# Weight blocks and degree counts moved beside a gather, last-stage masks and sums kept in PSUM, squares on ScalarE

## The chip, the cores and the metric

One core of a Trainium2 chip runs the whole program. The metric is the device time of one execution in microseconds (us). Of the kernel before there are three plain runs and one execution under the hardware profiler.

## The reference, cut to what matters

A graph of 100000 nodes with 32 features each (x) and 25000 edges (src, dst sorted, a type of 86, a weight). Four graph layers stand one behind the other, each with a residual and a layer norm over the 32 features:

```
x = layernorm(x + L0(x))   # 10 propagation steps: f = 0.9 * dn * segsum((f*sn)[src], dst) + 0.1 * x
x = layernorm(x + L1(x))   # 4-head attention over the edges of one src, softmax, mean over heads, + bias
x = layernorm(x + L2(x))   # relation layer: basis products, tanh gate, segment sum over dst, relu
x = layernorm(x + L3(x))   # L3(x) = segsum(x[src] * weight, dst) + x
```

Nodes without edges go through the norms alone.

## The kernel before, in words

The 25000 edges lie over 128 partitions with T = 196 edges each, in order of dst. XS and XD hold the rows of x for the source and for the target of each edge. They come by indirect DMAs from GpSimd's queue (POOL), one instruction for one edge column: 128 rows of 32 floats. XS takes 196 such instructions, the node table 196, XD 196. XD's are issued in three portions that fill gaps of POOL's order: columns 0 to XD_EARLY (148) ahead of the gather for list 0, up to XD_MID (186) behind it, and the last ten behind the payload gather.

Only edges whose source row is itself a target can change over the propagation steps. They are put on lists: list 0 has 7 trips here, list 1 has 2 trips, a trip being two halves of CU = 4 columns. `list_gather` (L1516) works a list: VectorE (DVE) fills the index tile cidx for both halves, POOL issues four indirect gathers for a half, DVE waits for their landing, takes the rows and refills the indices of the half for the next trip. What is given as `between` runs on DVE after the first two fills and ahead of the first take. There are two halves, so POOL is never more than eight gathers ahead of DVE.

The order around the first part of the change, on DVE: `sums_of_dst` makes segment sums by 32 scans (L1354) into the tile S; they are copied into FULL (L1688), which has 36 floats for an edge; SyncE (SP) writes FULL to the table full_d (L637). DVE waits for that write, clears the region with a memset of 7200 floats (L1712), and works list 0 from full_d. Then it puts out the list sums (L1722 to L1726); SP writes them and the payload. DVE next builds the weight blocks (L1735 to L1769) and the counts per target (L1773 to L1775), makes list 1 (`make_list`, L1465), and gathers its payload in two trips (L1777, `pay_take`). Some masks and a memset of S later it starts the gather of list 1 from the written list sums (L1792). All propagation steps follow, each waiting for the one ahead.

The last stage puts out the rows by target. It has ROUNDS = 7 rounds of RC = 28 edge columns. In a round DVE expands listed rows in a window (L2177 to L2187), adds them to XS (`add_listed`, L2210), and `out_dst` (L2216) norms XS, multiplies with the edge weight, makes 32 scans of 28 elements into S (L2230), adds twice XD, keeps a part for a row split over partitions (held, L2235), and norms again. `deviation` (L2202) squares on DVE (L2204), sums, and has ScalarE (ACT) take the root. `out_fill` writes half a round's 14 rows into the ring, and POOL scatters them to the output, one indirect DMA for a column (L911). The ring has two halves; a half is filled again when its scatters of the round ahead have landed (s_land). ACT's side of the roots is `take_roots` (L2305).

Of the kernel before, what the change touches and what calls it, by code (L numbers as in the profile page):

```python
# [5 lines left out]
ALU = mybir.AluOpType  # L6
# [62 lines left out]
def gnn_resnorm(nc, x, src, dst, etype, eweight, w1, fc_w, fc_b, bias1, w2, w_comp, w_self, A1w, A1b, A2w, A2b,  # L69
# [53 lines left out]
    with ctx:  # L123
# [304 lines left out]
        ROWS_AHEAD = 8  # L428
        XS_AHEAD, XD_EARLY, XD_MID = 160, 148, 186
        assert CH % 4 == 0 and NG == 7 * ROUNDS == 4 * (SINGLES - 1) + 1 and SINGLES <= 2 * ROUNDS  # L430
# [508 lines left out]
        def mid(ap, n):  # L939

            return ap.unsqueeze(1).to_broadcast([ap.shape[0], n, ap.shape[1]])

        @block.vector
        def _(dve):
# [711 lines left out]
            def carry_run(flat, flags, w=D, last=False):  # L1656

                with rn.trip_loop(2) as i:
# [8 lines left out]

            sums_of_dst = lambda src3, dst3, flat: segment_sums(src3, dst3, D, dmask, dfirst,
                                                                enter=lambda first: carry_run(flat, first))
            spread_of_dst = lambda ends_only=False: spread_back(  # L1670
# [12 lines left out]
            st.seq(V.tensor_tensor(Y3, XS3, bc3(c2[:, :], D), ALU.mult))  # L1683
            sums_of_dst(Y3, S3, S)
            st.do(V.memset(tm[:, :], 1.0))
            st.wait()
            positions(cs, act0, T, dmask, dfirst, tm[:, 0:1])
            st.do(V.tensor_copy(FULL[:, :, 0:D], S3))  # L1688
            st.do(V.tensor_copy(FULL[:, :, D], lcnt[:, 0:T]))
# [19 lines left out]
            st.do(V.tensor_copy(p0[:, :, 3], lq[:, 0:CW]))  # L1709
            dve.wait_ge(s_fullw, 16)  # L1710
            st.do(V.memset(zr[:, :, :], 0.0))
            st.do(V.memset(RB[:, 0:CW * TW], 0.0))  # L1712
            st.wait()
            list_gather(0, cs, 0, lidx2, row_take(0, cs, TW, RB[:, 0:CW * TW], TW, YW, True), 9)

# [18 lines left out]

            for k in range(2):  # L1735
                st.seq(V.tensor_tensor(prod[:, 0:NH * D].rearrange("p (h o) -> p h o", h=NH),
                                       wcat[:, :].rearrange("p (h o) -> p h o", h=NH),
                                       mid(wsd[:, k * D:(k + 1) * D], NH), ALU.mult))
                st.seq(V.tensor_reduce(ua[:, k, :], prod[:, 0:NH * D].rearrange("p (h o) -> p h o", h=NH), AX.X,
                                       ALU.add))  # L1740
            for k in range(2):
                for h in range(NH):
                    m = (k * NH + h) * D
                    st.do(V.tensor_scalar(udiag[:, m:m + D], ident[0:D, 0:D], ua[0:D, k, h:h + 1], None, ALU.mult))
            for j in range(GT):
                r = slice(32 * j, 32 * j + 32)

                st.do(V.tensor_scalar(bd1[r, j * NH * D:(j + 1) * NH * D].rearrange("i (o h) -> i o h", h=NH),
                                      wcat[r, :].rearrange("i (h o) -> i o h", h=NH), 1.0 / NH, None, ALU.mult))

                st.wait()
                st.do(V.tensor_reduce(bdm[r, j * D:(j + 1) * D], bd1[r, j * NH * D:(j + 1) * NH * D].rearrange(
                    "i (o h) -> i o h", h=NH), AX.X, ALU.add))
                for part, w in ((w16[r, 0:NB * D].rearrange("i (o b) -> i o b", b=NB),
                                 wf[r, :].rearrange("i (b o) -> i o b", b=NB)),
                                (w16[r, NB * D:(NB + 1) * D], aw[r, 0:D]),
                                (w16[r, (NB + 1) * D:(NB + 2) * D], aw[r, 2 * D:3 * D])):
                    st.seq(V.tensor_copy(part, w))
                    if j >= 2:
                        st.seq(V.tensor_tensor(part, w, part, ALU.subtract))  # L1760
                st.do(V.tensor_copy(bdy[r, j * D:(j + 1) * D], aw[r, D:2 * D]))

            st.seq(V.tensor_tensor(relf[:, NB:RW], relf[:, NB:RW], b_b2[:, :], ALU.add))
            st.seq(V.tensor_copy(rel3[:, 0, :], relf[:, :]))
            for k in range(2):
                st.seq(V.tensor_tensor(relf[:, :], relf[:, :], rel3[:, k, :], ALU.subtract))
                st.seq(V.tensor_copy(rel3[:, k + 1, :], relf[:, :]))
            st.wait()
            dve.sem_inc(s_wb, 1)  # L1769


            ones_t = ones[:, 0:1].to_broadcast([P, T]).unsqueeze(2)
            segment_sums(ones_t, c3[:, :].unsqueeze(2), 1, dmask, dfirst)  # L1773
            spread_back(c3[:, :].unsqueeze(2), 1, dend, dstf)
            dve.sem_inc(s_sri, 1)  # L1775
            cs = make_list(1, t1w, CW, pb[:, 0:1], float(CW - ZROW))
            list_gather(1, cs, 0, lq, pay_take(1, cs), 1)  # L1777
            list_masks(1)
# [422 lines left out]

            def deviation(x3):  # L2202

                st.seq(V.tensor_tensor(sq3, x3, x3, ALU.mult))  # L2204
                dve.sem_inc(tick, 1)
                st.seq(V.tensor_reduce(half, sq3, AX.X, ALU.add))
                root()
                st.seq(V.reciprocal(inv, half))

            def add_listed(i, y):  # L2210

                xs = chunk(XS, i)
                st.seq(V.tensor_tensor(y, y, cols2(act0, i).unsqueeze(2).to_broadcast([P, RC, D]), ALU.mult))
                st.seq(V.tensor_tensor(xs, xs, y, ALU.add))

            def out_dst(i, y):  # L2216

                part = prods[:, :, :].rearrange("p a b -> p (a b)")[:, 0:RC * D].rearrange("p (t d) -> p t d", d=D)
                sums, xs, xd = (chunk(t, i) for t in (S, XS, XD))
                center(xs)  # L2220
                deviation(xs)
                st.seq(V.tensor_tensor(inv, inv, cols2(ew, i), ALU.mult))
                st.seq(V.tensor_tensor(y, xs, bc3(inv, D), ALU.mult))
                if not (isinstance(i, int) and i == 0):

                    last = S[:, bass.ds(i * (RC * D) - D, D)]
                    st.seq(V.scalar_tensor_tensor(out=y[:, 0, :], in0=last, scalar=dmask[:, bass.ds(i * RC, 1)], in1=y[:, 0, :],
                                                  op0=ALU.mult, op1=ALU.add))
                for d in range(D):
                    st.do(V.tensor_tensor_scan(sums[:, :, d], cols2(dmask, i), y[:, :, d], 0.0, ALU.mult, ALU.add))  # L2230
                st.wait()
                dve.sem_inc(tick, 1)
                st.seq(V.scalar_tensor_tensor(out=xd, in0=xd, scalar=2.0, in1=sums, op0=ALU.mult, op1=ALU.add))

                st.seq(V.tensor_tensor(part, xd, cols2(held, i).unsqueeze(2).to_broadcast([P, RC, D]), ALU.mult))  # L2235
                st.seq(V.tensor_reduce(rowsq, part.rearrange("p t d -> p d t"), AX.X, ALU.add))
                st.seq(V.tensor_tensor(row, row, rowsq, ALU.add))
                center(xd)
                deviation(xd)

# [26 lines left out]
            out_fill(1, 0)  # L2267
            with st.loop(ROUNDS - 2, 2 * NEAR + 54) as k:
                y = expand_window(k + 2)
                dve.wait_ge(s_land[1], k * LAND + LAND)  # L2270
                dve.sem_inc(tick, 1)
                out_fill(k + 2, 1, ago=1)
                add_listed(k + 2, y)
                out_dst(k + 2, y)
                dve.wait_ge(s_land[0], k * LAND + 2 * LAND)
                dve.sem_inc(tick, 1)
                out_fill(k + 2, 0)

            def held_row():

                st.seq(V.tensor_scalar(tl[:, :], S3[:, T - 1, :], 0.0, None, ALU.add))
                carries()
# [16 lines left out]
        def _(act):  # L2299
# [274 lines left out]
            norm_acts(XD, sq_2)  # L2574
            take_roots(("norm",), 2 * ROUNDS + 1)

        @block.tensor
        def _(pe):
# [105 lines left out]
            carry(dcar, D)  # L2684
            column_row(6)
            carry(dcar, 1)
            carry(dbak, 1)
            column_row(7)
            carry(dcar, D)
# [165 lines left out]
```

## Time and profile before

| | |
|---|---|
| median of three runs | 2567.63 us (2566.56 to 2570.95) |
| profiled execution, own time | 2568.24 us |
| its span, first to last instruction | 2566.5 us |
| VectorE busy | 1897.8 us (74%), 3513 instructions |
| GpSimd busy | 1702.5 us (66%), 1727 instructions |
| ScalarE busy | 601.7 us (23%) |
| chain that ended last | VectorE 36%, issue 23%, GpSimd 16%, DMA 11% |

The busy shares are means over stages with different limits. In the timeline an instruction stands with its start, its duration, its line and, in brackets, how long its engine sat idle before it and what ended that. "issue" means that nothing in the profile shows a wait. Times below are us from the span's start.

### The profile page before, as it was taken

How to read it: one execution, taken by the hardware profiler on the slowest of the kernel's cores; microseconds unless marked ns; L12 is line 12 of the kernel's file. 1: busy time of each engine (PE TensorE's matmuls, PEld its weight loads, DVE VectorE, ACT ScalarE, POOL GpSimd, SP SyncE). 2: the span in 40 equal slices, each digit the busy share in tenths (PEclk: the TensorE clock that was granted, in tenths of full speed). 3: DMA queues.
4: the chain of work that ended last, by engine and by line, in shares of the span. 5: the costliest groups of instructions: out<-in, count | busy, mean ns of one | idle time of the engine just before them, and what ended most of it. 6: DMA issues, size and time to landing. Idle time of an engine off the chain costs nothing.

```text
span 2566.5 us, 24471 instructions
## 1 busy us (share of the span) xinstructions
PE 521.3 (20%) x3579; PEld 333.9 (13%) x3579; DVE 1897.8 (74%) x3513; ACT 601.7 (23%) x1410; POOL 1702.5 (66%) x1727
## 2 busy tenths in 40 slices
PE   5771000068100000000000303540045652000000
PEld 2330000057100000000000301430022321000000
DVE  7776888888874565663689967738789999888871
ACT  7992332223000000000000301541244441200000
POOL 6777767777747766664665767767367660665776
PEclk9996555589555555555555656555555555555555
DMA  7002333200012113322223120111100000210000
GB/s 244 13 12 72 96 97 101 75 13 13 12 64 14 34 13 26 31 27 15 83 54 69 25 69 12 7 36 37 54 8 8 9 9 1 70 15 7 10 9 9
DMA packets 100320, 100.95 MB, mean 39 GB/s; under 512 B 58360, under 2 KB 91304, under 8 KB 98480
## 3 DMA queue, kind: packets, MB, share of 16 engines
q0 software_dynamic: 53664, 20.91, 9.3%
q1 hardware_dynamic: 46288, 79.40, 8.6%
q14 instruction: 42, 0.34, 0.0%
q10 hardware_dynamic: 320, 0.20, 0.0%
q8 instruction: 6, 0.10, 0.0%
HBM read 38.06 MB, written 60.81 MB: 39 GB/s over the span
## 4 chain that ended last, share of the span: by engine, by line
DVE 36%; issue 23%; POOL 16%; DMA 11%; DVEq 3%; PE 2%; ACT 1%; POOLq 1%; SPq 0%; ACTq 0%
POOL ring L778 6%; POOL cring L471 3%; DMA cring<-sums_by_list,cidx 2%; POOL out_dram L911 2%; DMA cring<-sums_by_edge,cidx 1%; DVE RB L1230 1%; POOL attention_by_edge L876 1%; POOL attention_by_edge L795 1%; DVE banks L1111 1%; DVE banks L1101 1%; DVE SW L1107 1%; DVE SW L1116 1%; DVE SW L1106 1%; DVE SW L1354 1%; DVE banks L1095 1%
## 5 line engine op out<-in xcount | busy, mean ns | idle before, releaser
L480 POOL DMA_INDIRECT XS<-in_x_dram,xsi x196 | 199.2, 1017 | 70.1 <-issue 62.4
L480 POOL DMA_INDIRECT SW<-node_table,srci x196 | 200.4, 1022 | 66.1 <-issue 66.1
L480 POOL DMA_INDIRECT XD<-in_x_dram,xdi x196 | 196.0, 1000 | 62.5 <-issue 62.5
L911 POOL DMA_INDIRECT out_dram<-ring,ridx x168 | 175.6, 1045 | 74.1 <-issue 50.4
L471 POOL DMA_INDIRECT cring<-sums_by_list,cidx x128 | 123.8, 967 | 86.0 <-issue 76.0
L895 POOL DMA_INDIRECT out_dram<-z4w,oidx x112 | 111.9, 999 | 80.6 <-ACT oidx L2518 47.2
L2595 PE MATMUL banks<-YW 128*128 128x392 f16 x784 | 139.6, 332 | 46.0 <-ACT YW L2337 45.9
L2677 PE MATMUL banks<-tl,dcar 128*128 128x32 f32 (+1 forms) x14 | 4.4, 405 | 699.9 <-DVEq L1343 523.5
L778 POOL DMA_INDIRECT ring<-rgcn_table,aidx x56 | 56.2, 1003 | 102.9 <-DMA aidx<-rows 86.0
L778 POOL DMA_INDIRECT ring<-x_by_edge,aidx x96 | 91.4, 952 | 48.4 <-issue 43.7
L1014 DVE TENSOR_SCALAR YW<-YW,b_d 128x784 f16<-128x784 f16 x196 | 82.8, 423 | 46.9 <-PE banks L2595 45.0
L2822 PE MATMUL banks<-w,xw 128*128 128x512 f16 x196 | 90.2, 566 | 78.1 <-DVEq L2109 49.2
L895 POOL DMA_INDIRECT out_dram<-e4w,oidx x84 | 84.0, 1000 | 31.9 <-issue 23.8
L2677 PEld LDWEIGHTS banks<-tl,dcar 128*128 128x128 f32 x14 | 3.5, 312 | 702.2 <-DVEq L1343 525.2
L2595 PEld LDWEIGHTS banks<-YW 128*128 128x128 f16 x784 | 73.9, 98 | 112.0 <-issue 65.9
L814 POOL DMA_INDIRECT repeated_edges_by_src<-ring,aidx x64 | 68.0, 1063 | 30.3 <-issue 15.9
L1015 DVE TENSOR_SCALAR YW<-YW,b_s 128x784 f16<-128x784 f16 x196 | 82.7, 422 | 0.0
L2424 ACT ACTIVATE banks<-xw 128x896 f32<-128x896 f32 x7 | 6.4, 921 | 322.8 <-DVEq L1815 322.8
L471 POOL DMA_INDIRECT cring<-sums_by_edge,cidx x56 | 52.9, 945 | 42.0 <-DVE cidx L1519 28.6
L2330 ACT ACTIVATE YW<-iota_h,a_d 128x128 f16<-128x128 f16 x196 | 76.4, 390 | 6.1
L2330 ACT ACTIVATE YW<-iota_h,a_s 128x128 f16<-128x128 f16 x196 | 75.6, 386 | 0.0
L2312 ACT ACTIVATE roots<-roots,eps_norm 128x56 f32<-128x56 f32 x15 | 5.1, 341 | 290.1 <-DVEq L1071 290.1
(624 smaller groups left out, 3310.7 us busy)
## 6 DMA issues: line engine op xcount, KB each, us to landing
SW<-in_x_dram SPq DMA_DIRECT2D x20, 625.0 KB
out_dram<-SW SPq DMA_DIRECT2D x20, 625.0 KB
sums_by_list<-RB SPq DMA_DIRECT2D x2, 1800.0 KB
sums_by_edge<-RB SPq DMA_DIRECT2D x1, 3528.0 KB, 9.8
sums_by_list<-RB SPq DMA_DIRECT2D x2, 1600.0 KB
XS<-in_x_dram,xsi POOLq DMA_INDIRECT x196
list_values_by_edge<-RB SPq DMA_DIRECT2D x1, 3136.0 KB
attention_by_edge<-RB SPq DMA_DIRECT2D x1, 3136.0 KB
```

The costliest lines, as they stand in the source:

```text
L471: pool.indirect_dma_start(out=row, out_offset=None, in_=table, in_offset=off).then_inc(s_lland[v][h], 16)
L480: pool.indirect_dma_start(out=dest[:, t * w:(t + 1) * w], out_offset=None, in_=table, in_offset=bass.IndirectOffsetOnAxis(ap=idx[:, t:t + ...
L778: pool.indirect_dma_start(out=ring_row(h, j, D), out_offset=None, in_=table, in_offset=bass.IndirectOffsetOnAxis(ap=aidx[:, h, j:j + 1], a ...
L795: pool.indirect_dma_start(out=table, out_offset=bass.IndirectOffsetOnAxis(ap=aidx[:, h, j:j + 1], axis=0), in_=ring_row(h, j, w), in_offse ...
L814: pool.indirect_dma_start(out=table, out_offset=bass.IndirectOffsetOnAxis(ap=aidx[:, h, j:j + 1], axis=0), in_=ring_row(h, j, w), in_offse ...
L895: pool.indirect_dma_start(out=out[:, :], out_offset=bass.IndirectOffsetOnAxis(ap=oidx[:, j * GT + t:j * GT + t + 1], axis=0), in_=oring_ro ...
L911: pool.indirect_dma_start(out=out[:, :], out_offset=bass.IndirectOffsetOnAxis(ap=index(j), axis=0), in_=row(j), in_offset=None, bounds_che ...
L1014: V.tensor_scalar(oh_lo[0][:, j, :], iota_w, col(b_d), None, ALU.is_equal)
L1015: V.tensor_scalar(oh_lo[1][:, j, :], iota_w, col(b_s), None, ALU.is_equal).then_inc(s_oh, 1)
L2330: last = A.activation(hi_far[:, j, k * P:(k + 1) * P], iota_h[:, 0:P], ACT.Abs, bias=t[:, bass.ds(i * 4 + j, 1)])
L2595: last = M.matmul(bank[2 * k + h][:, 0:HH], oh_hi[b][:, j, k * P:(k + 1) * P], oh_lo[k][:, j, h * HH:(h + 1) * HH], start=False, stop=False)
L2822: M.matmul(bank[c][:, :], x16[:, b, c * P:(c + 1) * P], w16[:, 0:NB * D], start=True, stop=True).then_inc(s_msg, 1)
```

## The change

- The first segment sums are scanned straight into FULL, with a row width of 36 instead of 32; the copy goes.
- The wait for the write of FULL and the memset become the `between` of list 0's gather, so the first index fills stand ahead of them.
- `make_list` of list 1 goes ahead of the weight blocks and the counts, which become the `between` of the payload gather. TensorE's order follows (column_row(7) two places earlier).
- XD's portions become 162, 22 and 12 columns, from 148, 38 and 10.
- In the last stage the masks act0, held and dmask are copied once into PSUM banks and the sums of a round live in PSUM. ACT makes the two squares of a round, asked for by their own semaphores, and the roots likewise.

```
-        XS_AHEAD, XD_EARLY, XD_MID = 160, 148, 186
+        XS_AHEAD, XD_EARLY, XD_MID = 160, 162, 184
...
-            sums_of_dst(Y3, S3, S)
+            sums_of_dst(Y3, FULL[:, :, 0:D], RB[:, 0:T * TW], TW)
...
-            st.do(V.tensor_copy(FULL[:, :, 0:D], S3))
...
-            dve.wait_ge(s_fullw, 16)
-            st.do(V.memset(zr[:, :, :], 0.0))
-            st.do(V.memset(RB[:, 0:CW * TW], 0.0))
-            st.wait()
-            list_gather(0, cs, 0, lidx2, row_take(0, cs, TW, RB[:, 0:CW * TW], TW, YW, True), 9)
+            st.wait()
+            def clear_sums():
+                dve.wait_ge(s_fullw, 16)
+                st.do(V.memset(zr[:, :, :], 0.0))
+                st.do(V.memset(RB[:, 0:CW * TW], 0.0))
+                st.wait()
+            list_gather(0, cs, 0, lidx2, row_take(0, cs, TW, RB[:, 0:CW * TW], TW, YW, True), 9, clear_sums)
...
+            cs = make_list(1, t1w, CW, pb[:, 0:1], float(CW - ZROW))
+            def weights_and_counts():
+...
-            cs = make_list(1, t1w, CW, pb[:, 0:1], float(CW - ZROW))
-            list_gather(1, cs, 0, lq, pay_take(1, cs), 1)
+            list_gather(1, cs, 0, lq, pay_take(1, cs), 1, weights_and_counts)
...
-            def deviation(x3):
-                st.seq(V.tensor_tensor(sq3, x3, x3, ALU.mult))
+            act0_p, held_p, dmask_p = bank[6][:, 0:T], bank[6][:, 256:256 + T], bank[7][:, 256:256 + T]
+            sums = v3(pairs[2][:, 0:RC * D])
+            st.do(V.tensor_copy(act0_p, act0[:, :]))
+            st.do(V.tensor_copy(held_p, held[:, :]))
+            st.seq(V.tensor_copy(dmask_p, dmask[:, :]))
+            sq0, rt0 = nsquare[0], nroot[0]
+            def deviation(i, m):
+                dve.sem_inc(s_sqw, 1)
+                dve.wait_ge(s_sqr, i * 2 + (sq0 + m + 1))
                 dve.sem_inc(tick, 1)
                 st.seq(V.tensor_reduce(half, sq3, AX.X, ALU.add))
-                root()
+                dve.sem_inc(s_rtw, 1)
+                dve.wait_ge(s_rtr, i * 2 + (rt0 + m + 1))
+                dve.sem_inc(tick, 1)
                 st.seq(V.reciprocal(inv, half))
...
-                st.seq(V.tensor_tensor(y, y, cols2(act0, i).unsqueeze(2).to_broadcast([P, RC, D]), ALU.mult))
+                st.seq(V.tensor_tensor(y, y, cols2(act0_p, i).unsqueeze(2).to_broadcast([P, RC, D]), ALU.mult))
...
-                    st.do(V.tensor_tensor_scan(sums[:, :, d], cols2(dmask, i), y[:, :, d], 0.0, ALU.mult, ALU.add))
+                    st.do(V.tensor_tensor_scan(sums[:, :, d], cols2(dmask_p, i), y[:, :, d], 0.0, ALU.mult, ALU.add))
...
-                st.seq(V.tensor_tensor(part, xd, cols2(held, i).unsqueeze(2).to_broadcast([P, RC, D]), ALU.mult))
+                st.seq(V.tensor_tensor(part, xd, cols2(held_p, i).unsqueeze(2).to_broadcast([P, RC, D]), ALU.mult))
...
-            take_roots(("norm",), 2 * ROUNDS + 1)
+            half = roots[:, 0:RC]
+            for i in range(ROUNDS):
+                for m, t in enumerate((XS, XD)):
+                    act.wait_ge(s_sqw, nsquare[0] + 2 * i + m + 1)
+                    A.activation(sq_s[:, 0:RC * D], t[:, i * RC * D:(i + 1) * RC * D], ACT.Square).then_inc(s_sqr, 1)
+                    act.wait_ge(s_rtw, nroot[0] + 2 * i + m + 1)
+                    A.activation(half, half, ACT.Sqrt, scale=ROOTS["norm"][0] / D,
+                                 bias=eps_t["norm"][:, 0:1]).then_inc(s_rtr, 1)
+            take_roots(("norm",), 1)
```

## Rows read from the trace of the kernel before

**Rows 1.** POOL's timeline, 735 to 920: start, duration, line, tiles, idle before.
```profile
736.96 0.94 POOL L480 DMA_INDIRECT XD<-in_x_dram,xdi  x1 [0.30 <-issue]
762.65 0.94 POOL L471 DMA_INDIRECT cring<-sums_by_edge,cidx  x1 [24.75 <-DVE cidx L1519]
...
884.51 0.94 POOL L471 DMA_INDIRECT cring<-payload,cidx  x1 [3.49 <-DVE cidx L1519]
...
903.24 0.94 POOL L471 DMA_INDIRECT cring<-payload,cidx  x1 [0.30 <-issue]
...
918.58 0.94 POOL L471 DMA_INDIRECT cring<-sums_by_list,cidx  x1 [1.82 <-DVE cidx L1519]
```

**Rows 2.** VectorE's timeline, 739 to 918.
```profile
739.71 3.43 DVE L1688 COPY RB<-SW 128x6272 f32<-128x6272 f32 x1
...
755.58 6.06 DVE L1712 MEMSET RB<- 128x7200 f32 x1 [1.45 <-issue]
...
853.39 0.29 DVE L1736 TENSOR_TENSOR prods<-wcat,wsd 128x128 f32<-128x128 f32 x1 [0.25 <-DVE z4w L1723]
...
874.80 0.36 DVE L1188 TENSOR_REDUCE tl<-t1w 128x1 f32<-128x200 f32 x1
...
883.54 0.24 DVE L1519 TENSOR_SCALAR cidx<-RB 128x4 int32<-128x4 int32 x2
...
906.57 0.17 DVE L1552 TENSOR_SCALAR e4w<-cring 128x16 f32 x1 [4.54 <-DMA cring<-payload,cidx]
...
917.60 0.24 DVE L1519 TENSOR_SCALAR cidx<-RB 128x4 int32<-128x4 int32 x2
```

**Rows 3.** DMA issues: queue, operation, count, size, median us to landing.
```profile
sums_by_edge<-RB SPq DMA_DIRECT2D x1, 3528.0 KB, 9.8
...
payload<-z4w SPq DMA_DIRECT2D x1, 400.0 KB, 2.6
```

**Rows 4.** SyncE's queue, timeline 700 to 960.
```profile
858.83 0.34 SPq L652 DMA_DIRECT2D payload<-z4w  x1
```

**Rows 5.** POOL's timeline in the last stage.
```profile
2328.90 0.98 POOL L911 DMA_INDIRECT out_dram<-ring,ridx  x1 [21.88 <-DVE ridx L2245]
...
2395.26 1.26 POOL L911 DMA_INDIRECT out_dram<-ring,ridx  x1 [0.30 <-DVE ridx L2245]
...
2412.32 1.84 POOL L911 DMA_INDIRECT out_dram<-ring,ridx  x1 [0.31 <-issue]
...
2520.93 0.98 POOL L911 DMA_INDIRECT out_dram<-ring,ridx  x1 [0.30 <-issue]
...
2555.68 0.98 POOL L911 DMA_INDIRECT out_dram<-ring,ridx  x1 [0.31 <-issue]
```

**Rows 6.** VectorE's timeline in the last stage.
```profile
2361.23 0.98 DVE L2177 COPY RB<-YW 128x1376 f32 x1
...
2394.64 1.03 DVE L2177 COPY RB<-YW 128x1376 f32 x1
...
2406.89 0.62 DVE L2244 TENSOR_TENSOR ring<-XD,banks 128x448 f32<-128x448 f32 x1 [4.96 <-DMA out_dram<-ring,ridx]
...
2412.21 1.09 DVE L2204 TENSOR_TENSOR RB<-XS 128x896 f32 x1
...
2415.20 0.34 DVE L2208 RECIPROCAL banks<-roots 128x28 f32<-128x28 f32 x1 [0.66 <-ACT roots L2312]
```

**Rows 7.** ScalarE's timeline: a square of 896 elements.
```profile
2191.11 0.95 ACT L2368 ACTIVATE prods<-XD 128x896 f32<-128x896 f32 x1 [2.54 <-DVEq L1434]
```

**Rows 8.** VectorE by line and form: count, busy us, mean ns, idle before.
```profile
L1956 DVE TENSOR_TENSOR_SCAN e4w<-t,z4w 128x200 f32<-128x200 f32 x4 | 2.0, 556 | 0.0
L1354 DVE TENSOR_TENSOR_SCAN e4w<-banks,z4w 128x200 f32<-128x200 f32 x4 | 2.0, 554 | 0.0
L1431 DVE TENSOR_REDUCE banks<-XD 128x28 f32<-128x896 f32 x21 | 23.0, 1095 | 0.7
L1438 DVE TENSOR_REDUCE roots<-prods 128x28 f32<-128x896 f32 x12 | 13.0, 1086 | 0.7
```

More of the change, by code:

```diff
@@ L1666, in carry_run @@
                     dve.sem_inc(tick, 1)
-            sums_of_dst = lambda src3, dst3, flat: segment_sums(src3, dst3, D, dmask, dfirst,
-                                                                enter=lambda first: carry_run(flat, first))
+            sums_of_dst = lambda src3, dst3, flat, w=D: segment_sums(src3, dst3, D, dmask, dfirst,
+                                                                     enter=lambda first: carry_run(flat, first, w))
             spread_of_dst = lambda ends_only=False: spread_back(
@@ L1732, in _ @@
             trips0 = cs.trips
[L1735 to L1749, printed above, removed]
-                st.wait()
[L1752 to L1767, printed above, removed]
-            st.wait()
-            dve.sem_inc(s_wb, 1)
-            ones_t = ones[:, 0:1].to_broadcast([P, T]).unsqueeze(2)
-            segment_sums(ones_t, c3[:, :].unsqueeze(2), 1, dmask, dfirst)
@@ L1774, in _ @@
-            spread_back(c3[:, :].unsqueeze(2), 1, dend, dstf)
-            dve.sem_inc(s_sri, 1)
-            cs = make_list(1, t1w, CW, pb[:, 0:1], float(CW - ZROW))
-            list_gather(1, cs, 0, lq, pay_take(1, cs), 1)
+            cs = make_list(1, t1w, CW, pb[:, 0:1], float(CW - ZROW))
+            def weights_and_counts():
+                for k in range(2):
+                    st.seq(V.tensor_tensor(prod[:, 0:NH * D].rearrange("p (h o) -> p h o", h=NH),
+                                           wcat[:, :].rearrange("p (h o) -> p h o", h=NH),
+                                           mid(wsd[:, k * D:(k + 1) * D], NH), ALU.mult))
+                    st.seq(V.tensor_reduce(ua[:, k, :], prod[:, 0:NH * D].rearrange("p (h o) -> p h o", h=NH), AX.X,
+                                           ALU.add))
+                for k in range(2):
+                    for h in range(NH):
+                        m = (k * NH + h) * D
+                        st.do(V.tensor_scalar(udiag[:, m:m + D], ident[0:D, 0:D], ua[0:D, k, h:h + 1], None, ALU.mult))
+                for j in range(GT):
+                    r = slice(32 * j, 32 * j + 32)
+                    st.do(V.tensor_scalar(bd1[r, j * NH * D:(j + 1) * NH * D].rearrange("i (o h) -> i o h", h=NH),
+                                          wcat[r, :].rearrange("i (h o) -> i o h", h=NH), 1.0 / NH, None, ALU.mult))
+                    st.wait()
+                    st.do(V.tensor_reduce(bdm[r, j * D:(j + 1) * D], bd1[r, j * NH * D:(j + 1) * NH * D].rearrange(
+                        "i (o h) -> i o h", h=NH), AX.X, ALU.add))
+                    for part, w in ((w16[r, 0:NB * D].rearrange("i (o b) -> i o b", b=NB),
+                                     wf[r, :].rearrange("i (b o) -> i o b", b=NB)),
+                                    (w16[r, NB * D:(NB + 1) * D], aw[r, 0:D]),
+                                    (w16[r, (NB + 1) * D:(NB + 2) * D], aw[r, 2 * D:3 * D])):
+                        st.seq(V.tensor_copy(part, w))
+                        if j >= 2:
+                            st.seq(V.tensor_tensor(part, w, part, ALU.subtract))
+                    st.do(V.tensor_copy(bdy[r, j * D:(j + 1) * D], aw[r, D:2 * D]))
+                st.seq(V.tensor_tensor(relf[:, NB:RW], relf[:, NB:RW], b_b2[:, :], ALU.add))
+                st.seq(V.tensor_copy(rel3[:, 0, :], relf[:, :]))
+                for k in range(2):
+                    st.seq(V.tensor_tensor(relf[:, :], relf[:, :], rel3[:, k, :], ALU.subtract))
+                    st.seq(V.tensor_copy(rel3[:, k + 1, :], relf[:, :]))
+                st.wait()
+                dve.sem_inc(s_wb, 1)
+                ones_t = ones[:, 0:1].to_broadcast([P, T]).unsqueeze(2)
+                segment_sums(ones_t, c3[:, :].unsqueeze(2), 1, dmask, dfirst)
+                spread_back(c3[:, :].unsqueeze(2), 1, dend, dstf)
+                dve.sem_inc(s_sri, 1)
@@ L2218, in out_dst @@
                 part = prods[:, :, :].rearrange("p a b -> p (a b)")[:, 0:RC * D].rearrange("p (t d) -> p t d", d=D)
-                sums, xs, xd = (chunk(t, i) for t in (S, XS, XD))
+                xs, xd = (chunk(t, i) for t in (XS, XD))
                 center(xs)
-                deviation(xs)
+                deviation(i, 0)
                 st.seq(V.tensor_tensor(inv, inv, cols2(ew, i), ALU.mult))
@@ L2224, in out_dst @@
                 if not (isinstance(i, int) and i == 0):
-                    last = S[:, bass.ds(i * (RC * D) - D, D)]
-                    st.seq(V.scalar_tensor_tensor(out=y[:, 0, :], in0=last, scalar=dmask[:, bass.ds(i * RC, 1)], in1=y[:, 0, :],
-                                                  op0=ALU.mult, op1=ALU.add))
+                    st.seq(V.scalar_tensor_tensor(out=y[:, 0, :], in0=sums[:, RC - 1, :], scalar=dmask[:, bass.ds(i * RC, 1)],
+                                                  in1=y[:, 0, :], op0=ALU.mult, op1=ALU.add))
                 for d in range(D):
-                    st.do(V.tensor_tensor_scan(sums[:, :, d], cols2(dmask, i), y[:, :, d], 0.0, ALU.mult, ALU.add))
+                    st.do(V.tensor_tensor_scan(sums[:, :, d], cols2(dmask_p, i), y[:, :, d], 0.0, ALU.mult, ALU.add))
                 st.wait()
@@ L2238, in out_dst @@
                 center(xd)
-                deviation(xd)
+                deviation(i, 1)
             def out_fill(i, h, ago=0):
@@ L2267, in _ @@
             out_fill(1, 0)
-            with st.loop(ROUNDS - 2, 2 * NEAR + 54) as k:
+            with st.loop(ROUNDS - 2, 2 * NEAR + 50) as k:
                 y = expand_window(k + 2)
@@ L2279, in held_row @@
             def held_row():
-                st.seq(V.tensor_scalar(tl[:, :], S3[:, T - 1, :], 0.0, None, ALU.add))
+                st.seq(V.tensor_scalar(tl[:, :], sums[:, RC - 1, :], 0.0, None, ALU.add))
                 carries()
@@ L2685, in _ @@
             column_row(6)
+            column_row(7)
             carry(dcar, 1)
             carry(dbak, 1)
-            column_row(7)
             carry(dcar, D)
```

## The prediction

> **What bounds the kernel now.** I read the chain of waits first. It passes between VectorE (DVE), GpSimd's indirect DMAs (POOL) and the landings, so a piece of work counts only where its neighbours wait for it. Then I read POOL's and DVE's timelines of the two stretches that the diff touches, side by side.
>
> In the first stretch POOL is done with XD's early columns at 737.9 and sits idle for 24.75 us, until DVE fills the first indices of list 0 [rows 1]. DVE meanwhile copies the sums (3.43), waits for the write to land, and clears 7200 floats [rows 2]. The reader is to see that the memset has an "issue" of 1.45 ahead of its 6.06. I take both as its price, 7.5, though the clearing is needed only at the first take. Later DVE works from 853.39 to 874.80 on weights and counts, then 8.7 us on the list; only then does POOL start the payload, at 884.51, and DVE waits through the gather until 906.57 [rows 1, 2].
>
> In the last stage POOL is the bound. From 2328.90 it scatters without a gap. The last 27 steps, with DVE idle, take 34.75 us, 1.287 each; the 140 steps from 2328.90 to 2520.93 take 192.03 where 140 x 1.287 is 180.2 [rows 5]. So 11.8 us are stalls inside POOL's instructions. The two long ones shown begin while DVE is in an operation with two SBUF tensors (the square, L2204) or in an SBUF copy (L2177); the first ends its extra 0.86 about 0.97 after the square's start [rows 5, 6]. A DVE round is 2394.64 - 2361.23 = 33.4, POOL's is 28 x 1.287 = 36.0 without stalls, and DVE waits 4.96 for landings [rows 6].
>
> **The change, part by part.**
>
> List 0. The copy's 3.43 goes, but POOL decides. A gather step is (903.24 - 884.51) / 15 = 1.249 [rows 1]. Fourteen more XD columns keep POOL busy to 737.9 + 17.5 = 755.4. Small DVE operations newly beside them may delay it; I take 0.8 with the step to the gather: 756.2. The write of the sums waits for the copy; DVE goes on from its landing at 755.58 - 1.45 = 754.1, so 3.4 earlier is 750.7 [rows 2], ahead of 756.2. The memset then ends near 758.2, and the first half lands no sooner than 756.2 + 4 x 1.249 = 761.2, so it is covered. If that cover were gone, its 7.5 would be back. Start of the gather 762.65 -> 756.2: **6.4 us**. The write beside XD gathers has no row; its landing costs nothing up to 5.5 late, and at twice its 9.8 [rows 3] the start is 760.5 and the memset ends at 768, which leaves about 2 of the 6.4.
>
> Payload. DVE's chain from the gather's start to 853.39 is untouched, so `make_list` starts at 853.39 - 6.4 = 847.0. From 874.80 to POOL's start at 884.51 are 9.7, so the payload gather starts at 856.7 [rows 1, 2]. XD's 22 middle columns are done by 756.2 + (56 + 22) x 1.249 = 853.6. The payload's write goes at 858.83 - 6.4 = 852.4 and lands 2.6 later, 855.0 [rows 3, 4]. Neither is late. DVE's fills end at 856.0, and weights and counts take 874.80 - 853.39 = 21.4, to 877.4. This is where I don't follow the plain reading that 21.4 vanish: POOL may issue only two halves, eight gathers or 10 us, and then waits for the first take and refill. Take, refill and the step to POOL I put at 1.3 (an estimate from the 0.17 of a take and the 0.97 from fill to POOL's start [rows 1, 2]): 878.7. Eight gathers more have their last start at 878.7 + 7 x 1.249 = 887.4, and its take follows after 906.57 - 903.24 = 3.3, at 890.8 against 906.57: **15.8** so far, of which this edit gives 9.4.
>
> List 1's gather. DVE's fill comes 917.60 - 906.57 = 11.0 behind the last take, POOL 0.98 behind that: 890.8 + 12.0 = 902.8. POOL has twelve XD columns now: 887.4 + 13 x 1.249 = 903.6. POOL is last, by 0.8. Start 918.58 -> 903.6: **14.9 us** stay [rows 1, 2]. All behind it waits in a chain for its predecessor, so I carry 14.9 to the last stage.
>
> Last stage. The three mask copies stand where DVE waits for rows before the first round: nothing. A square on ACT is 0.95 [rows 7]. The hand-over both ways is 0.66 less the root's own 0.3, so about 0.3 [rows 6]: 1.25 against 1.09 + 0.15 on DVE. I take nothing; 0 to 0.2 a square. Scans with their mask in PSUM cost 554 ns against 556 with all in SBUF, a result in PSUM costs 1095 against 1086 [rows 8]: I take nothing, and 32 x 0.009 = 0.3 a round as the upper bound. Only one round of DVE stands ahead of POOL's run, so these ends are worth below 1 us.
>
> What the edit buys are the stalls. The squares leave DVE, and the products with act0 and held, the scans and the sum into XD keep one SBUF tensor each. Left are XS + y (L2214) and the window's copy (L2177). If each caught POOL at its worst in five rounds, 5 x (0.97 + 0.9) = 9.4 would stay; at best 0. The copy's stall is 0.28 in the row shown, and the phase of XS + y behind the landing puts it just between two of POOL's starts. I take 2.6: 11.8 - 2.6 = **9.2 us**. POOL's round becomes 36.5, still above DVE's 33.4.
>
> The Trainium skill, page "VectorE: DVE Perf Modes", section "The TRN2 errata — SBUF-src ops pay a fixed extra latency per instruction", speaks against the PSUM masks: it gives a fixed 120 cycles for a PSUM source against 58 for SBUF. By it some 35 instructions a round would be about 65 ns longer each (an estimate from that page), 2.3 us once, and the sum 21.8. The two scan rows [rows 8] don't bear it out.
>
> **The sum:** 14.9 + 9.2 = 24.1. On the profiled execution's own 2568.24 (span 2566.5) that is 2544.1; the median of the runs is 0.6 lower. **I predict 2543.5.**
>
> **Rivals.**
>
> *The stalls come back.* XS + y and the copy meet POOL at new phases: 9.4 stay, 2.4 are won. For it: each stall moves POOL's phase. Against: DVE starts each later round from a landing, so the phase repeats. 2567.6 - 14.9 - 2.4 = 2550.3.
>
> *List 0 is not freed earlier.* The large write and the gathers share DMA engines, it lands at 760.5, and the memset delays the first take: 2 of 6.4 are won. For it: nothing of this size stands beside XD gathers in the rows. Against: it has 5.5 us to spare. 2567.6 - 10.5 - 9.2 = 2548.
>
> *PSUM is dear for short scans, and the kernel is slower.* No row has a scan of 28 elements into PSUM. With x us more in a DVE round, the first round costs x. From x = 3.1 DVE bounds the other five, with 33.4 + x each against 38.4 now. The last stage gets longer by 6x - 25, so all of 14.9 is lost at x = 6.7, 0.2 us a scan. At x = 7.8 it gives 2567.6 - 14.9 + 21.8 = 2574.5. For it: strided writes to PSUM here are unseen. Against [rows 8], with 0.009 for a result in PSUM. The page named above has the same direction with a third of the decisive price.
>
> *More is won.* No stall stays and POOL's XD runs smoothly: 14.9 + 11.8 + 1 = 27.7, 2540.
>
> **How the numbers follow.** Forecast (2540 to 2548) 0.66, stalls back 0.13, list 0 not freed 0.08, more won 0.08, slower 0.03, and 0.02 for a change that does nothing measurable. A measurement of this kernel tells about 0.2%, 5 us, from no change. The first four cases are all faster by more than that: faster 0.95, same 0.02, slower 0.03. The range holds the forecast, both smaller gains and the larger one, with some 3 us about the outer ones for what a moved chain may lose or gain elsewhere: 2537 to 2553.
>
> **What would show it.** Right: the first sums_by_edge gather near 756, the payload's near 857 with a pause of some 12 us behind its eighth gather, the sums_by_list gather near 903.6, and the last stage's first ring scatter about 15 earlier. In the last stage POOL's 140 steps take 183, not 192. Wrong: a first take later than its landing in list 0; scans L2230 spaced wider than 0.13; DVE waiting for no landing in the late rounds; POOL starts inside XS + y. The largest risk is the phase of the two operations left.

## The result and the profile after

The changed kernel takes 2539.88 us (median of 4 runs, 2537.83 to 2540.46) against 2567.60 us: ratio 0.9888, 95% interval 0.9871 to 0.9906, so 27.7 us less (24 to 33). Predicted were 2543.5 and 24.1. The profiled execution took 2539.72, its span 2538.0, 28.5 less than that of before.

POOL's timeline from 754 to 903 answers to [rows 1].

```profile
754.40 0.94 POOL L480 DMA_INDIRECT XD<-in_x_dram,xdi  x1 [0.30 <-issue]
755.65 0.94 POOL L471 DMA_INDIRECT cring<-sums_by_edge,cidx  x1 [0.30 <-issue]
...
855.28 0.94 POOL L471 DMA_INDIRECT cring<-payload,cidx  x1 [2.11 <-DVE cidx L1519]
...
864.14 0.94 POOL L471 DMA_INDIRECT cring<-payload,cidx  x1 [0.30 <-issue]
877.84 0.94 POOL L471 DMA_INDIRECT cring<-payload,cidx  x1 [12.75 <-DVE cidx L1519]
...
901.65 0.95 POOL L480 DMA_INDIRECT XD<-in_x_dram,xdi  x1 [0.30 <-DVE cidx L1519]
902.90 0.94 POOL L471 DMA_INDIRECT cring<-sums_by_list,cidx  x1 [0.30 <-issue]
```

The 24.75 us of idling ahead of list 0's gather are gone: it follows the last of 162 XD columns after the usual 0.30. The payload gather starts 29 earlier, but stops behind its eighth transfer for 12.75 us. List 1's gather follows POOL's own columns, so POOL is the last to be ready. VectorE's timeline answers to [rows 2].

```profile
747.14 0.24 DVE L1519 TENSOR_SCALAR cidx<-RB 128x4 int32<-128x4 int32 x2
752.64 0.19 DVE L1714 MEMSET zr<- 128x160 f32 x1 [5.25 <-DMA sums_by_edge<-RB]
754.28 6.06 DVE L1715 MEMSET RB<- 128x7200 f32 x1 [1.45 <-issue]
...
761.97 0.17 DVE L1579 TENSOR_SCALAR RB<-cring 128x4 f32 x1 [1.64 <-DMA cring<-sums_by_edge,cidx]
...
876.52 0.17 DVE L1552 TENSOR_SCALAR e4w<-cring 128x16 f32 x1 [0.91 <-DVE c L1389]
...
884.68 0.34 DVE L1552 TENSOR_SCALAR e4w<-cring 128x16 f32 x1 [6.96 <-DMA cring<-payload,cidx]
...
889.91 0.17 DVE L1552 TENSOR_SCALAR e4w<-cring 128x16 f32 x1 [4.53 <-DMA cring<-payload,cidx]
```

Read the wait in front of 761.97: the clearing ended at 760.34 and VectorE still waited 1.64 for the landing, so the 7.5 us are covered, with 1.6 to spare. After 876.52 VectorE waits 6.96 and 4.53: the work beside the gather was done while POOL stood still, and POOL then works while VectorE stands still.

POOL's timeline in the last stage answers to [rows 5], VectorE's to [rows 6].

```profile
2310.10 0.98 POOL L911 DMA_INDIRECT out_dram<-ring,ridx  x1 [21.27 <-DVE ridx L2262]
...
2408.49 1.16 POOL L911 DMA_INDIRECT out_dram<-ring,ridx  x1 [0.30 <-issue]
...
2492.43 0.98 POOL L911 DMA_INDIRECT out_dram<-ring,ridx  x1 [0.30 <-issue]
...
2527.17 0.98 POOL L911 DMA_INDIRECT out_dram<-ring,ridx  x1 [0.30 <-issue]
```

```profile
2383.82 0.62 DVE L2261 TENSOR_TENSOR ring<-XD,banks 128x448 f32<-128x448 f32 x1 [2.95 <-DMA out_dram<-ring,ridx]
...
2390.29 1.09 DVE L2222 TENSOR_REDUCE roots<-RB 128x28 f32<-128x896 f32 x1 [1.18 <-ACT RB L2596]
2391.93 0.34 DVE L2226 RECIPROCAL banks<-roots 128x28 f32<-128x28 f32 x1 [0.55 <-ACT roots L2598]
...
2394.24 3.52 DVE L2247 TENSOR_TENSOR_SCAN banks<-banks,RB 128x28 f32<-128x28 f32 x32
...
2408.04 0.62 DVE L2261 TENSOR_TENSOR ring<-XD,banks 128x448 f32<-128x448 f32 x1 [0.23 <-DVE banks L2226]
...
2408.66 0.87 DVE L2185 COPY RB<-YW 128x1376 f32 x1
```

The 140 steps from the first scatter take 2492.43 - 2310.10 = 182.33, not 192.03. Five scatters of the 168 are longer than 1.0 us, 0.82 in all, where before 24 were, 10.5 in all; 2408.49 is one of the five, begun while VectorE fills the ring's slot (2408.04) right ahead of the window's copy. VectorE still waits 2.95 for a landing ahead of 2383.82, so POOL is still the bound of the stage. The square on ScalarE costs VectorE 1.18 where its own took 1.09 and a step.

### The profile page after: what moved, and what is told of

Its sections match the earlier page's. It is cut to its first block, busy times and chain, and to the rows that moved or that the text cites. A ratio compares the mean times of both kernels' runs of the same rounds, so it can differ in the third digit from the quotient of the medians.

```text
span 2538.0 us, 24265 instructions
## 1 busy us (share of the span) xinstructions
PE 525.0 (21%) x3579; PEld 335.1 (13%) x3579; DVE 1875.5 (74%) x3501; ACT 615.7 (24%) x1424; POOL 1688.4 (67%) x1727
## 4 chain that ended last, share of the span: by engine, by line
POOL 41%; issue 29%; DVE 15%; DMA 10%; DVEq 2%; PE 1%; POOLq 1%; ACT 0%; SPq 0%; ACTq 0%
POOL SW L480 8%; POOL XS L480 8%; POOL XD L480 6%; POOL ring L778 6%; POOL out_dram L911 5%; POOL cring L471 3%; DMA cring<-sums_by_list,cidx 2%; POOL attention_by_edge L876 1%; DVE RB L1230 1%; POOL attention_by_edge L795 1%; DMA cring<-sums_by_edge,cidx 1%; POOL ring L869 1%; DMA ring<-YW 1%; DMA ring<-attention_table,aidx 1%; DVE YW L1230 1%
## 5 line engine op out<-in xcount | busy, mean ns | idle before, releaser
L911 POOL DMA_INDIRECT out_dram<-ring,ridx x168 | 165.9, 987 | 73.5 <-issue 51.9
L778 POOL DMA_INDIRECT ring<-appnp_table,aidx x56 | 52.9, 945 | 28.2 <-issue 17.9
L869 POOL DMA_INDIRECT ring<-attention_table,aidx x56 | 55.4, 988 | 23.4 <-issue 14.6
## 6 DMA issues: line engine op xcount, KB each, us to landing
sums_by_edge<-RB SPq DMA_DIRECT2D x1, 3528.0 KB, 10.7
```

The lines of the kernel that those rows point to most:

```text
L778: pool.indirect_dma_start(out=ring_row(h, j, D), out_offset=None, in_=table, in_offset=bass.IndirectOffsetOnAxis(ap=aidx[:, h, j:j + 1], a ...
L869: pool.indirect_dma_start(out=ring_row(h, j, D), out_offset=None, in_=att_d[:, :], in_offset=bass.IndirectOffsetOnAxis(ap=aidx[:, h, j:j + ...
L911: pool.indirect_dma_start(out=out[:, :], out_offset=bass.IndirectOffsetOnAxis(ap=index(j), axis=0), in_=row(j), in_offset=None, bounds_che ...
```

## The experiments

Each kernel was timed in five rounds against the kernel before on the same chip; "gain" is the difference of these medians. Before took 2568.99, 2565.76 and 2570.17 in the three groups of runs, so gains are compared, not times. The interval of a gain reaches 3 to 5 us to either side; where two gains differ by less, the timelines decide.

**1 and 2. Each part alone.** The two kernels share out the hunks of the diff: all down to line 1800 with the PE order in one, the last stage in the other.

> The first five edits alone (sums scanned into the write's tile, clearing beside the list 0 gather, 162/22/12 columns of XD, list 1 before weights and counts); the last stage is that of the kernel before. Theory (two separate gains, the first about 17 to 18 by the trace of after, which has the first ring scatter 18.8 earlier, less some 0.8 for the first round): 2567.6 - 17.5 = 2550, first ring scatter 18 earlier than before, POOL's 140 steps 192 as before. Rival (the 14.9 of the prediction is the real gain, and the 3 us above it are drift between two executions): 2552.7. Rival (the last stage's stalls depend on what arrives earlier): 140 steps of another length than 192.

> The last-stage edits alone (masks and sums in PSUM, squares on ScalarE). Theory (POOL bounds that stage and loses its stalls, 9.7, and the first round is some 0.8 shorter): 2567.6 - 10.5 = 2557, 140 steps in 182.3. Rival (the gain comes from VectorE's shorter round, which had 5 us of waiting in each): at most 1, so 2566.7, 140 steps near 192 and longer waits of VectorE for landings. If the two parts add up, the gains of these two kernels sum to 27.7.

Measured: 2549.30, ratio 0.9924 (0.9910 to 0.9937), gain 19.7; and 2557.79, ratio 0.9955 (0.9942 to 0.9969), gain 11.2. The sum, 30.9, agrees with 27.7 within the intervals. POOL's timelines, first and 141st ring scatter of the first and of the second kernel:

```profile
2314.08 0.98 POOL L911 DMA_INDIRECT out_dram<-ring,ridx  x1 [21.87 <-DVE ridx L2253]
...
2506.40 0.98 POOL L911 DMA_INDIRECT out_dram<-ring,ridx  x1 [0.30 <-issue]
```

```profile
2330.19 0.98 POOL L911 DMA_INDIRECT out_dram<-ring,ridx  x1 [21.36 <-DVE ridx L2254]
...
2512.62 0.98 POOL L911 DMA_INDIRECT out_dram<-ring,ridx  x1 [0.30 <-issue]
```

That is 192.3 against 182.4 for the 140 steps. The stalls don't depend on when the stage begins, and the last-stage edits alone remove them. VectorE's shorter round as the source (at most 1 us) falls. One expectation was missed: the first kernel's first ring scatter comes 14.8 earlier than before, not 18; from its list 1 gather to that scatter it takes 1410.7, before 1410.3. The profiled execution was the longest of the five, 2553.76. For the 3 us between theory and rival the medians (a gain of 16 to 23) and this timeline thus disagree, and whether they are gain or drift stays open.

**3 and 4. Which of the last-stage edits.**

```diff
-                dve.sem_inc(s_sqw, 1)
-                dve.wait_ge(s_sqr, i * 2 + (sq0 + m + 1))
+                st.seq(V.tensor_tensor(sq3, x3, x3, ALU.mult))
```

> The kernel after with the squares back on VectorE as products of an SBUF tensor with itself; masks and sums stay in PSUM. Theory (a GpSimd indirect DMA that starts within a two-SBUF-input VectorE operation is held until about 0.97 after that operation's start): the stalls of the two squares come back, 0.86 and 0.18 a round before, 5 rounds: 5 us, 2545, 140 steps in 187. Rival (the PSUM masks and sums hold the gain): 2540, 140 steps in 182.

Measured: 2545.41, ratio 0.9903 (0.9888 to 0.9918), gain 23.6, 4.1 less than the whole change; 140 steps in 188.71. POOL's timeline has the first and the 141st scatter:

```profile
2310.72 0.98 POOL L911 DMA_INDIRECT out_dram<-ring,ridx  x1 [21.21 <-DVE ridx L2261]
...
2499.43 0.98 POOL L911 DMA_INDIRECT out_dram<-ring,ridx  x1 [0.30 <-issue]
```

The timelines of both engines show a held scatter, VectorE's row and POOL's:

```profile
2392.63 1.09 DVE L2220 TENSOR_TENSOR RB<-XS 128x896 f32 x1
...
2392.68 1.89 POOL L911 DMA_INDIRECT out_dram<-ring,ridx  x1 [0.30 <-issue]
```

It ends 1.94 after the square's start: 0.97 until it is let go, and its own 0.97. The four other scatters held by a square of XS in this trace end 1.94 or 1.95 after theirs. These five make about 4.5 of the 6.4 that came back in the steps; the rest is mostly in scatters that now begin in XS + y, the slot's fill or the copy, because the phase has moved.

```diff
-                st.seq(V.tensor_tensor(y, y, cols2(act0_p, i).unsqueeze(2).to_broadcast([P, RC, D]), ALU.mult))
+                st.seq(V.tensor_tensor(y, y, cols2(act0, i).unsqueeze(2).to_broadcast([P, RC, D]), ALU.mult))
```

(so for dmask, held and the sums)

> The kernel after with act0, held, dmask and the sums of a round back in SBUF; the squares stay on ScalarE. Theory: the sum into XD and the product with held (0.62 and 0.05 to 0.59 a round before) hold POOL again: about 4.5 us, 2544.5, 140 steps in 187; scans 0.121 apart, not 0.110. Rival (the squares alone made the gain): 2540.5, 140 steps in 182.5.

Measured: 2542.57, ratio 0.9894 (0.9879 to 0.9909), gain 26.4; 140 steps in 183.76. POOL's timeline:

```profile
2312.31 0.98 POOL L911 DMA_INDIRECT out_dram<-ring,ridx  x1 [22.76 <-DVE ridx L2258]
...
2496.07 0.98 POOL L911 DMA_INDIRECT out_dram<-ring,ridx  x1 [0.30 <-issue]
```

Only 1.4 came back, not 4.5. The theory of the mechanism stands (eight of the ten held scatters in this trace begin in the act0 product or the copy, the two others are held by at most 0.05 in the scans), but with the squares away POOL's starts fall elsewhere, and the sum into XD no longer meets one. Of the 9.7, taking back the squares loses 6.4 and taking back the masks and sums 1.4. The other 1.9 either edit wins without the other: the squares on ScalarE alone bring 192.0 to 183.8, the masks and sums in PSUM alone to 188.7.

The scans by line and form (count, busy us, mean ns, idle before), in the changed kernel and with the masks in SBUF:

```profile
L2247 DVE TENSOR_TENSOR_SCAN banks<-banks,RB 128x28 f32<-128x28 f32 x224 | 24.6, 199 | 0.8
```

```profile
L2243 DVE TENSOR_TENSOR_SCAN SW<-dmask,RB 128x28 f32 x160 | 20.5, 208 | 0.6
```

24.6 / 224 is 0.110 us each, 20.5 / 160 is 0.128 (the other 64 scans of this kernel, in two of the rounds, take 0.122): with mask and result in PSUM the scan is the cheaper one.

**5 and 6. The first part taken apart.** The list 0 edits alone:

> Only the list 0 edits and the 162/22/12 columns; weights and counts stay ahead of the payload's list, the last stage is that of before. Theory (each step of the first part is kept by the next): list 0 gather at 755.6, payload gather 7 earlier than before's 884.5, list 1 gather 7 earlier than 918.4; time of before less 7 to 8. The payload edit then has the other 8 of the 15. Rival (an earlier list 0 runs into the middle columns or the payload's write): the payload gather stays later than 880 and the gain is below 4.

Measured: 2556.71, ratio 0.9964 (0.9950 to 0.9977), gain 9.1. The list 0 gather starts at 756.22, the payload's at 877.38, list 1's at 912.49. POOL's timeline:

```profile
912.49 0.94 POOL L471 DMA_INDIRECT cring<-sums_by_list,cidx  x1 [0.30 <-issue]
```

The payload's gather is 7.1 earlier than before, list 1's, behind POOL's own twelve columns, 6.1; so about 6 of the 15 are list 0's, 9 the payload's. The gain is 3 us more than these 6; in this trace the stretch from list 1's gather to the ring is shorter by 4 (1406.1 against 1410.3), though nothing in it was edited. Then the clearing put back in front:

```diff
+            clear_sums()
-            list_gather(0, cs, 0, lidx2, row_take(0, cs, TW, RB[:, 0:CW * TW], TW, YW, True), 9, clear_sums)
+            list_gather(0, cs, 0, lidx2, row_take(0, cs, TW, RB[:, 0:CW * TW], TW, YW, True), 9)
```

> The kernel after, with the clearing of the row tile again ahead of the list 0 gather's first indices. Theory (it is covered only because it stands beside POOL's first gathers): VectorE fills the indices at 760.4, POOL starts at 761.4 instead of 755.6, and 5.8 us come back whole: 2539.9 + 5.8 = 2545.7. Rival (the removed copy and the columns alone made the gain): below 1.5, 2541.

Measured: 2542.82, ratio 0.9910 (0.9895 to 0.9925), gain 22.9, 4.8 less than the whole change. VectorE's timeline:

```profile
760.49 0.24 DVE L1519 TENSOR_SCALAR cidx<-RB 128x4 int32<-128x4 int32 x2
...
767.73 0.17 DVE L1579 TENSOR_SCALAR RB<-cring 128x4 f32 x1 [7.01 <-DMA cring<-sums_by_edge,cidx]
```

The take is 5.76 later than 761.97, and list 1's gather, at 908.63, 5.73 later: nothing between absorbs it. Moving the clearing under the gather is thus most of what list 0 gave.

**7. The held instruction elsewhere.**

```diff
-            st.seq(V.tensor_tensor(Y3, XS3, bc3(c2[:, :], D), ALU.mult))
+            st.seq(V.tensor_copy(pfirst[:, 0:T], c2[:, :]))
+            st.seq(V.tensor_tensor(Y3, XS3, bc3(pfirst[:, 0:T], D), ALU.mult))
```

> The kernel after, with the multiplier of the 6272-element product XS times c2 copied into PSUM first (196 elements). A test of the held POOL instruction away from the edited places: POOL's DMA at 710.8 lasts 6.99 us and ends with that product. Theory (two SBUF inputs hold POOL): no instruction of POOL beyond 1.7 there, the list 0 gather 6 earlier, 749.7 to 752 (the write of the sums lands near 752); the first take then waits for the clearing, which ends at 760.3, so only 1.6 are won: 2538. Rival (any long VectorE operation holds POOL): the 6.99 stays, 2540. By the Trainium skill's page VectorE: DVE Perf Modes, section The TRN2 errata, a PSUM source costs 120 cycles instead of 58, 65 ns at most on one instruction, by an estimate from that page.

Measured: 2536.34, ratio 0.9888 (0.9873 to 0.9903), gain 29.4; the times don't tell it from 27.7. The timelines do, first that of the changed kernel, then that of this one:

```profile
710.23 6.69 DVE L1683 TENSOR_TENSOR YW<-XS,c 128x6272 f32<-128x6272 f32 x1
...
710.76 6.99 POOL L480 DMA_INDIRECT XD<-in_x_dram,xdi  x1 [0.30 <-issue]
```

```profile
709.69 6.69 DVE L1684 TENSOR_TENSOR YW<-XS,banks 128x6272 f32<-128x6272 f32 x1
...
709.82 0.94 POOL L480 DMA_INDIRECT XD<-in_x_dram,xdi  x1 [0.30 <-issue]
711.06 0.94 POOL L480 DMA_INDIRECT XD<-in_x_dram,xdi  x1 [0.30 <-issue]
...
753.11 0.94 POOL L471 DMA_INDIRECT cring<-sums_by_edge,cidx  x1 [4.33 <-DMA sums_by_edge<-RB]
```

The product lasts 6.69 either way; with one of its inputs in PSUM, POOL runs through it. That it is a long operation is not what holds POOL. The Trainium skill, page "SBUF — State Buffer", section "Who interferes with whom", says that a VectorE instruction with two SBUF inputs contends with a GpSimd instruction that reads SBUF; this trace agrees, 6.99 against 0.94. The list 0 gather started at 753.11, behind the landing of its table, only 2.5 earlier and not 6, and the first take was then bound by the clearing, 760.40.

**8 and 9. The pause in the payload gather.** The work beside the gather is cut around the first takes:

```diff
-            list_gather(1, cs, 0, lq, pay_take(1, cs), 1, weights_and_counts)
+            list_gather(1, cs, 0, lq, pay_take(1, cs), 1, lambda: weights((0, 1, 2)), (weights_end, counts))
...
+                if later:
+                    for h in range(2):
+                        half_trip(0, h)
+                        later[h]()
```

> The kernel after, with the work beside the payload gather cut in three: weights of blocks 0 to 2, then the first half's take and refill, block 3 and the rest of the weights, the second half's take and refill, then the counts, then the loop from the second trip. Theory (the pause of 12.75 us on POOL comes from its two slots, not from the amount of work): POOL's 16 payload gathers run with a pause below 1, the last take is at 877.5 instead of 889.9, POOL's last 12 columns end at 890.4 and the list 1 gather starts there instead of 902.9: 12.4 less, 2527.5. Rival (the landings, or something else that the counts feed, are next in line): the list 1 gather starts after 897 and less than 6 are won.

Measured: 2511.75, ratio 0.9787 (0.9774 to 0.9800), gain 54.0. That is 26 more than the change, twice what the theory gives. The peeled trip of this kernel refills its slots with the first trip's indices, so its second payload trip holds copies of the first: it leaves out the second trip's entries and is no form of the change to be used. The list 1 gather did start at 890.43, but its 128 gathers then took 267.6 us instead of 282.3, which neither theory had said. Next, the same cut with the second trip's indices.

> As the kernel split_weights, but the peeled first trip asks for the second trip's rows; in split_weights it asked for the first trip's rows a second time, so its second payload trip held copies of the first. Theory (the pause on POOL is worth 12.4, and the other 15 of that kernel came from list 1's passes, 282.3 to 267.6, because the copied entries no longer read the one zero row): list 1 gather at 890.4, its 128 gathers in 282 again, 2539.9 - 12.4 = 2527.5. Rival (the split itself makes the passes faster): 128 gathers in 267.6, 2512.

Measured: 2532.19, ratio 0.9846 (0.9833 to 0.9860), gain 38.0, 10.3 more than the change; 128 gathers in 283.5. POOL's timeline:

```profile
864.36 0.94 POOL L471 DMA_INDIRECT cring<-payload,cidx  x1 [0.30 <-issue]
865.61 0.94 POOL L471 DMA_INDIRECT cring<-payload,cidx  x1 [0.30 <-issue]
...
891.06 0.94 POOL L471 DMA_INDIRECT cring<-sums_by_list,cidx  x1 [0.30 <-issue]
```

No pause, and list 1's gather 11.8 earlier. In the profiled execution 1.1 of these went again to held scatters in the last stage (140 steps in 183.40: another phase), 1.1 to the 128 gathers, and 1.2 to a stage between that varies (below).

**10. What the accident had shown.** In the changed kernel the last batch of list 1's passes 2 to 8 lands 5.4 to 6.7 us after its last start (taken to VectorE's first use), the second of pass 1 after 2.7. Late batches are mostly padding (counted from the reference's inputs, at most 17 of the 128 partitions have an entry in list 1's last four columns), and all padding reads one zero row.

```diff
+            st.seq(V.tensor_scalar(lkey, lnext, float(ZROW), pneg[:, 0:1], ALU.is_ge, ALU.mult))
+            st.seq(V.tensor_tensor(lidx2, lnext, lkey, ALU.subtract))
-            st.seq(V.tensor_copy(lidx2, lnext))
```

> The kernel after, with 128 zero rows behind the list 1 table instead of one, and the padding entries of partition p reading zero row p in passes 2 to 8. Theory (many partitions that read one row of memory are served one after the other; the third and fourth batch of a pass, which hold the most padding, land 4.3 and 5.7 after their last start in after, 3.5 and 3.4 in split_weights): both near 2.8 to 3.5, 1.7 to 2.4 us less in each of 7 passes, the 128 gathers in 266 to 270 instead of 282, 2539.9 - 13 = 2527. Rival (rows read a second time land faster, and that is what helped split_weights): no change, 2540.

Measured: 2520.35, ratio 0.9802 (0.9789 to 0.9815), gain 49.8, 22 more than the change. The last start of a batch on POOL and its use on VectorE (timeline), in the changed kernel and here, both at the end of the sixth pass:

```profile
1108.91 0.94 POOL L471 DMA_INDIRECT cring<-sums_by_list,cidx  x1 [0.30 <-issue]
...
1114.85 0.29 DVE L1581 TENSOR_TENSOR y<-cring,e4w 128x128 f32<-128x128 f32 x1 [3.31 <-DMA cring<-sums_by_list,cidx]
```

```profile
1096.70 0.94 POOL L471 DMA_INDIRECT cring<-sums_by_list,cidx  x1 [0.30 <-issue]
...
1099.22 0.29 DVE L1582 TENSOR_TENSOR y<-cring,e4w 128x128 f32<-128x128 f32 x1 [1.97 <-DMA cring<-sums_by_list,cidx]
```

5.94 against 2.52. The last batch of pass 1, whose padding still reads one row, takes 4.4 here as there (4.5). The 128 gathers take 263.1, 19.2 less, and the scatter behind them starts another 3.2 sooner after them. I had expected 13, from the accident, perhaps because its copied entries still met one another; with a row for each partition the last batches land as early as the first ones. GpSimd's queue in the stretch of these gathers (DMA queue, kind: packets, MB, share of 16 engines), in the changed kernel from 902 to 1185 and here from 902 to 1167:

```profile
q0 software_dynamic: 5590, 2.21, 22.8%
```

```profile
q0 software_dynamic: 5650, 2.24, 6.2%
```

So the same bytes kept the DMA engines busy for a quarter of the time: the packets themselves became shorter. What makes reads of one row slow is not shown.

**11. All together**, with c2 in PSUM, 164/22/10 columns and list 0's padding spread too.

> The kernel after with all that helped: c2 in PSUM with 164/22/10 columns of XD, the weights cut around the payload takes, and zero rows spread over 128 rows for list 0 and for list 1's passes 2 to 8. Theory (the pieces stand one behind the other in one chain and add up): 1.6 + 12.4 + 13 + about 4 for list 0, whose last batches land 3.6, 4.5, 6.2 and 7.3 after their last start: 2539.9 - 31 = 2509. Rival (list 0 is bound by VectorE's takes, and POOL's columns hold the list 1 gather): no more than 27 together, 2513 or later.

Measured: 2502.18, ratio 0.9730 (0.9717 to 0.9743), gain 68.0. It beats both kernels, the changed one by 40. List 0's batches now all land 2.5 to 2.7 after their last start but the first, which waits for the clearing; its last three took 4.4, 6.1 and 7.3 in the changed kernel. Its last take is at 824.44 instead of 831.69.

## Why the prediction was right, and where it was off

*List 0, 6.4 us.* Forecast 756.2, measured 755.65, bound by POOL's columns as said. The cover was thinner than said: the write landed for VectorE at 752.6, not 750.7 (it took 10.7 instead of 9.8, and VectorE came to it 1.1 later than the copy's 3.43 alone would make it), so the clearing ended 2.1 later than forecast, and 1.6 us of room were left instead of 3.

*Payload, and the halved hope.* Start 856.7 forecast, 855.28 measured; restart 878.7 and 877.84; last take 890.8 and 889.91. Not to count the 21.4 us of work as gone was the right step. Experiment 9 shows that the two slots made the difference: with an earlier refill of each the pause is gone and list 1's gather starts 11.8 sooner.

*List 1, 14.9 us.* Forecast 903.6 with POOL last; measured 902.90 with POOL last. Over the four kernels of one code there (the changed one and experiments 1, 3, 4) it starts at 902.5 to 903.9, against 917.7 and 918.6 without: 15.0.

*Carried to the last stage: too little by 3 us here.* From list 1's gather to the first ring scatter the profiled execution took 1407.2, before 1410.3. VectorE's first round explains some 0.8, which I had put at "below 1" and left out of the sum. Another 0.9 are list 1's gathers (282.3 against 283.2), and 1.3 lie between the first scatter to the attention table and VectorE's first use of that table. POOL's timelines there, before and after:

```profile
1776.59 1.84 POOL L795 DMA_INDIRECT attention_table<-ring,aidx  x1 [0.30 <-issue]
...
1789.03 1.84 POOL L795 DMA_INDIRECT attention_table<-ring,aidx  x1 [0.30 <-issue]
```

```profile
1772.99 1.79 POOL L795 DMA_INDIRECT attention_table<-ring,aidx  x1 [0.30 <-DMA ring<-YW]
```

Of six scatters held there in before (five by the sum of XD and SW, two tensors in SBUF, one by a sum of the same kind) five are left, which is 0.9 of the 1.3. From the first of these scatters to the table's use it takes 75.5 to 75.9 in the six of the thirteen traces in which three of these scatters last over 1.5 us, and 76.7 to 77.0 in the seven in which four do, whatever was edited; what sets this phase stays open. In the ten traces whose list 1 reads the same rows the whole stretch takes 1404.6 to 1412.4, and the longest is that of experiment 2, which has the shorter first round. So beyond the first round's 0.8 no run shows that an edit won these 3 us; they may be drift. The interval of the ratio (24 to 33 us) doesn't tell 24.1 from 27.7.

*Last stage, 9.2 us.* The size was right (9.7, and 182.3 for the 140 steps where 183 was forecast), but two errors of the working cancelled. Of the 11.8 that I called stalls, 1.34 are a gap behind the 85th scatter (a step of 2.63 instead of 1.29) that every kernel here shows, edited or not; what it is stays open. Only 10.5 were stalls, and of these 0.82 remain, not 2.6: XS + y met POOL once, by 0.29, and four, by 0.05 to 0.18 each, begin in the slot's fill, which I hadn't listed; they all end 0.99 after the start of the copy behind it, and whether the fill or the copy holds them isn't settled. So "no stall stays", my rival at 2540, was nearer in this term. Its time was met too, but not by its sum: it counted 11.8 for this stage, and the stage gave 9.7.

*PSUM, taken as free.* The scans became cheaper, 3.52 us for 32 against 3.88 to 4.14, though mask and result moved together, so which of the two did it isn't told. The Trainium skill, page "VectorE: DVE Perf Modes", section "The TRN2 errata — SBUF-src ops pay a fixed extra latency per instruction", with 120 cycles for a PSUM source and 58 for SBUF, would have made them about 2 us a round dearer (an estimate from that page). The measurement decides: it has the other sign here, and the rival with the slower kernel had nothing to stand on.

## What to carry to other kernels

Work put beside a transfer queue is hidden only for as long as the queue's slots last: cut it where the slots want refilling, and the pause of 12.75 us is gone. Where GpSimd issues the transfers, take one of two SBUF inputs away from VectorE's operations (copy the small operand to PSUM, give the squares to ScalarE). That doesn't free POOL of everything: a plain SBUF copy held scatters before, 1.26 instead of 0.98 at 2395.26 [rows 5, 6]. Moving one such operation shifts the phase of the rest, so count held instructions over the whole stage, and look for a constant gap before calling all excess a stall. Let padding entries of a gather read rows of their own, not one common zero row.

## What the runs showed of the hardware that I had not expected

Gathers in which most partitions read the same row of memory land late: 5.94 us after the last start against 2.52 with a row for each partition, and up to 7.3 against 2.7 in list 0. It was worth 22 us in list 1 alone, almost as much as the whole change.

An indirect-DMA instruction of GpSimd that starts inside a VectorE product or sum with two SBUF inputs ends at that operation's start plus nearly its length plus its own 0.97: 1.94 us after the start of one of 1.09, and an instruction of 6.99 beside one of 6.69.
